# A graph attention and propagation kernel: a new order of the same instructions within a pipeline step

## The reference

```
h = x W_fc^T ;  f1 = h a1 ;  f2 = h a2
scores = leaky_relu(f1[:, None] + f2[None, :], 0.2), masked where adj == 0
attn = softmax(scores) ;  x = layernorm(x + elu(attn @ x))
xn = x / |x| ;  out = (xn xn^T) @ adj @ x ;  x = layernorm(x + out)
```

## Time and profile before

| what | value |
|---|---|
| median of three runs | 379.62 us |
| the profiled execution | 380.89 us, span 379.1 us |
| PE busy | 327.4 us (86%) |
| DVE busy | 330.5 us (87%) |
| ACT busy | 275.1 us (73%) |
| POOL busy | 194.7 us (51%) |
| moved by DMA | 42.41 MB, mean 112 GB/s |

### The profile page before, as it was taken

How to read it: one execution, slowest core, us unless ns; L and a number is a source line. 1 busy time by engine, 2 the same in 40 slices (tenths; PEclk the granted TensorE clock), 3 DMA queues, 4 the chain that set the end, 5 groups by cost and what they waited for, 6 DMA issues and landing times. The chain is left out here.

```text
span 379.1 us, 6926 instructions
## 1 busy us (share of the span) xinstructions
PE 327.4 (86%) x2244; PEld 302.6 (80%) x2244; DVE 330.5 (87%) x1012; ACT 275.1 (73%) x593; POOL 194.7 (51%) x167
## 2 busy tenths in 40 slices
PE   3095999899898989999898989989898989999790
PEld 1084999889797979889797979879797979998780
DVE  4589959999999999999999999999999999957412
ACT  0468696868878787868878787878878787884342
POOL 3405564654547375554548375554648475645401
PEclk9998799999999999999999999999999999999896
DMA  6861071534434544533443543633443541210102
GB/s 210 237 165 55 12 211 35 134 112 113 128 95 114 165 112 123 156 112 91 135 109 113 167 112 112 165 113 75 148 114 112 168 111 58 57 57 0 57 17 93
DMA packets 33971, 42.41 MB, mean 112 GB/s; under 512 B 1136, under 2 KB 25744, under 8 KB 33936
## 3 DMA queue, kind: packets, MB, share of 16 engines
q0 software_dynamic: 16896, 25.17, 24.6%
q1 hardware_dynamic: 17040, 16.81, 14.2%
HBM read 33.59 MB, written 8.39 MB: 111 GB/s over the span
## 5 line engine op out<-in xcount | busy, mean ns | idle before, releaser
L616 PE MATMUL ps_h<-x_hi,probT_hi 128*128 128x256 f32 x256 | 79.8, 312 | 0.4 <-issue 0.4
L617 PE MATMUL ps_h<-x_lo,probT_hi 128*128 128x256 f32 x256 | 72.8, 284 | 0.0
L618 PE MATMUL ps_h<-x_hi,probT_lo 128*128 128x256 f32 x256 | 72.6, 284 | 0.0
L600 PE MATMUL ps_probT<-ident,prob 128*128 128x128 f32 x256 | 41.6, 289 | 33.4 <-ACT prob L465 30.7
L646 PE MATMUL ps_l<-xn_hi,adj_sb 128*128 128x256 f32 x256 | 66.0, 297 | 2.1 <-POOL xn_lo L249 2.1
L600 PEld LDWEIGHTS ps_probT<-ident,prob 128*128 128x128 f32 x256 | 30.7, 148 | 43.8 <-ACT prob L465 35.2
L249 POOL TENSOR_TENSOR xn_lo<-xn,xn_hi 128x1024 fp32r<-128x1024 f32 x16 | 40.0, 2502 | 49.9 <-ACT xn_hi L499 49.9
L682 PE MATMUL ps_l<-w_sb,xnT 128*128 128x256 f32 x256 | 65.2, 380 | 0.3
L647 PE MATMUL ps_l<-xn_lo,adj_sb 128*128 128x256 f32 x256 | 63.3, 287 | 0.0
L669 PE MATMUL ps_l<-xn,z_sb 128*128 128x256 f32 x256 | 57.9, 379 | 0.0
L485 ACT ACTIVATE exp_h<-ps_h,rden 128x256 f32<-128x256 f32 x64 | 30.3, 474 | 36.9 <-PE ps_h L618 27.6
(11 more groups left out here) (52 smaller groups left out, 691.2 us busy)
## 6 DMA issues: line engine op xcount, KB each, us to landing
adj_sb<-adj POOLq DMA_DIRECT2D x16, 1024.0 KB, 5.9
x_sb<-x SPq DMA_DIRECT2D x16, 512.0 KB, 4.7
x_hi<-x POOLq DMA_DIRECT2D x16, 512.0 KB, 4.1
out<-o_sb SPq DMA_DIRECT2D x16, 512.0 KB, 3.1
attn_cols<-w_attn SPq DMA_DIRECT2D x2, 0.1 KB, 1.6
wfc<-w_fc SPq DMA_DIRECT2D x1, 32.0 KB, 1.7
```

Of the source, the lines that this page charges most:

```text
L600: last = nc.tensor.transpose(ps_probT[c % 2][:, k * P:(k + 1) * P], prob[:, c, k * P:(k + 1) * P], ident[:])
L616: nc.tensor.matmul(ps, probT_hi[:, c, blk], x_hi[n][:, k, :], start=(k == 0), stop=False)
L617: nc.tensor.matmul(ps, probT_hi[:, c, blk], x_lo[n][:, k, :], start=False, stop=False)
L618: last = nc.tensor.matmul(ps, probT_lo[:, c, blk], x_hi[n][:, k, :], start=False, stop=(k == NC - 1))
```

## The change

The four lists of calls are written in another order. Some calls change their index by one, as the loop's step boundary is at another place for that engine (on POOL `split_xn(i)` becomes `split_xn(i + 1)`, for example); each graph still gets each call once. `row_moments` and `row_moments2` are cut in two: the lines that add the epsilon are now functions of their own, `shifted_moments` and `shifted_moments2`, so that other calls can stand between. SP's list is as before. Waits, buffers, shapes and operations are the same.

```
 POOL
-                split_xn(i)
-                load_x_hi(i + 2)
-                norm(i)
                 load_adj(i + 3)
                 residual_sum(i + 1)
-                split_x(i + 2)
                 power2(i - 1)
+                load_x_hi(i + 3)
                 shift2(i - 1)
                 power(i + 1)
+                norm(i + 1)
+                split_xn(i + 1)
+                split_x(i + 3)

 DVE
                 last.then_inc(mv2_ok, 1)
+
+            def shifted_moments2(g):
+                if not graph(g):
+                    return
+                n = g % NBUF
                 dve.wait_ge(mv2_ok, g + 1)
...
-                residual2(i - 2, 1)
-                masked_f2(i + 1, 2)
-                negate_max(i + 1, 0)
+                masked_f2(i + 1, 3)
                 residual2(i - 2, 2)
                 residual2(i - 2, 3)
-                masked_f2(i + 1, 3)
-                node_scores(i + 2, 1)
+                negate_max(i + 1, 0)
+                negate_max(i + 1, 1)
+                node_scores(i + 2, 0)
                 residual(i)
-                negate_max(i + 1, 1)
                 row_moments2(i - 2)
                 probT_lo_part(i + 1, 0)
+                probT_lo_part(i + 1, 1)
+                shifted_moments2(i - 2)
                 row_moments(i)
-                node_scores(i + 2, 0)
-                probT_lo_part(i + 1, 1)
+                shifted_moments(i)
+                node_scores(i + 2, 1)
                 denominators(i + 1)
+                make_mask(i + 2)
                 normalise(i)
+                residual2(i - 1, 0)
                 probT_lo_part(i + 1, 2)
-                make_mask(i + 2)
+                masked_f2(i + 2, 0)
+                masked_f2(i + 2, 1)
                 probT_lo_part(i + 1, 3)
-                masked_f2(i + 2, 0)
-                residual2(i - 1, 0)
-                masked_f2(i + 2, 1)
+                masked_f2(i + 2, 2)
+                residual2(i - 1, 1)

 ACT (the new list; the old one is in the code above)
+                copy_xnT(i - 1, 0)
+                probT_hi_part(i + 1, 1)
+                lrelu(i + 1, 3)
+                copy_w(i - 1, 0)
+                copy_xnT(i - 1, 1)
+                softmax_exp(i + 1, 2)
+                softmax_exp(i + 1, 3)
+                copy_w(i - 1, 1)
+                normalise2(i - 2)
+                probT_hi_part(i + 1, 2)
+                elu_exp(i + 1, 0)
+                elu_relu(i + 1, 0)
+                elu_exp(i + 1, 1)
+                xn_hi_part(i)
+                probT_hi_part(i + 1, 3)
+                elu_relu(i + 1, 1)
+                lrelu(i + 2, 0)
+                elu_exp(i + 1, 2)
+                lrelu(i + 2, 1)
+                lrelu(i + 2, 2)
+                elu_relu(i + 1, 2)
+                elu_exp(i + 1, 3)
+                elu_relu(i + 1, 3)
+                scale_z(i, 0)
+                scale_z(i, 1)
+                softmax_exp(i + 2, 0)
+                softmax_exp(i + 2, 1)
+                scale_z(i, 2)
+                scale_z(i, 3)
+                probT_hi_part(i + 2, 0)

 PE (the new list)
+                bcast_f2(i + 1)
+                transpose_prob(i, 3)
                 attend(i, 2)
+                make_out(i - 2, 3)
                 attend(i, 3)
+                make_z(i - 1, 0)
+                make_z(i - 1, 1)
+                make_z(i - 1, 2)
+                make_z(i - 1, 3)
+                transpose_xn(i - 1, 0)
                 transpose_prob(i + 1, 0)
+                transpose_prob(i + 1, 1)
+                transpose_xn(i - 1, 1)
                 make_w(i - 1, 0)
                 make_w(i - 1, 1)
+                attend(i + 1, 0)
                 transpose_prob(i + 1, 2)
+                attend(i + 1, 1)
                 make_out(i - 1, 0)
                 make_out(i - 1, 1)
                 make_out(i - 1, 2)
```

More of the change, by code:

```diff
@@ L375, in row_moments, with shifted_moments @@
                 last.then_inc(mv_ok, 1)
+            def shifted_moments(g):
+                if not graph(g):
+                    return
+                n = g % NBUF
                 dve.wait_ge(mv_ok, g + 1)
@@ L539, in _ @@
             for i in STEPS:
[L540 to L556, removed]
                 copy_xnT(i - 1, 0)
-                softmax_exp(i + 1, 1)
+                probT_hi_part(i + 1, 1)
+                lrelu(i + 1, 3)
+                copy_w(i - 1, 0)
                 copy_xnT(i - 1, 1)
-                probT_hi_part(i + 1, 0)
-                copy_w(i - 1, 0)
                 softmax_exp(i + 1, 2)
-                lrelu(i + 1, 3)
+                softmax_exp(i + 1, 3)
                 copy_w(i - 1, 1)
-                probT_hi_part(i + 1, 1)
-                softmax_exp(i + 1, 3)
+                normalise2(i - 2)
                 probT_hi_part(i + 1, 2)
-                normalise2(i - 2)
                 elu_exp(i + 1, 0)
+                elu_relu(i + 1, 0)
[17 more added lines that the diff above has]
+                probT_hi_part(i + 2, 0)
         @block.tensor
@@ L686, in _ @@
             for i in STEPS:
+                bcast_f2(i + 1)
+                transpose_prob(i, 3)
                 attend(i, 2)
+                make_out(i - 2, 3)
                 attend(i, 3)
-                make_out(i - 2, 3)
-                for c in range(NC):
-                    make_z(i - 1, c)
+                make_z(i - 1, 0)
[3 more added lines that the diff above has]
+                transpose_xn(i - 1, 0)
                 transpose_prob(i + 1, 0)
-                for d in range(DC):
-                    transpose_xn(i - 1, d)
+                transpose_prob(i + 1, 1)
+                transpose_xn(i - 1, 1)
                 make_w(i - 1, 0)
                 make_w(i - 1, 1)
-                transpose_prob(i + 1, 1)
+                attend(i + 1, 0)
                 transpose_prob(i + 1, 2)
+                attend(i + 1, 1)
                 make_out(i - 1, 0)
-                attend(i + 1, 0)
                 make_out(i - 1, 1)
-                transpose_prob(i + 1, 3)
-                bcast_f2(i + 2)
-                attend(i + 1, 1)
                 make_out(i - 1, 2)
```

## The result

The changed kernel takes 357.01 us (median of 4 runs, 355.62 to 359.15) against 379.59: a ratio of 0.9415, 95% interval 0.9344 to 0.9486. In a second set it is 356.53 us, ratio 0.9425 (0.9387 to 0.9462). Forecast was 352 us in a range of 348 to 365.

What follows compares the result with a forecast made beforehand. DVE, held by POOL at L418, was taken to bound the kernel, with PE the bound afterwards. Twelve steps of 2.15 us, plus 2.6 at the end, minus 0.7 at the start, took 27.7 off 379.6: 352 us, range 348 to 365.

Steps and rivals of the forecast that it cites:

- The bound before was DVE, by a hold of L418: DVE is full in each 21.45 us step; its tiny epsilon addition takes 3.97 us, held while POOL works.
- PE becomes the bound, 19.3 us a step: With the new order PE never waits, so the step falls from 21.45 to 19.3 us.
- The floor: PE's own work per step: 21.45 less 2.16 us lost at two transposes of prob, 19.3 us.
- The hold at the new place: Moved shifted_moments2 on DVE meets POOL's residual sum: held 0 to 2.37 us, taken as 0.2.
- Early DVE part: Eight DVE operations reading PSUM run beside POOL's two splits; negate_max starts 4.8 to 5.4 us into the step.
- Late DVE part: DVE from node_scores to probT_lo 2, done at 19.2 us, needed by PE at 20.1; slack given as 0.7.
- The rule of the Trainium skill: Two-port or two-SBUF-input DVE instructions and SBUF-reading GpSimd ones block each other throughout; mask blocked until 15.8, sum unchanged.
- Start and end: Work before and after the twelve steps: start loses 0.7 us, allowing 4 either way; end gains 2.6.
- The sum: 12 x 2.15 + 2.6 - 0.7 = 27.7 us saved: span 351.4 us, median 352.
- adj lands late: Rival: adj, issued 6.8 us before its mask, arrives late; 380 to about 410 us; chance 0.03, plus 0.03 for no gain.
- Two holds for one: Rival: x_lo holds negate_max and residual sum holds L418; step 22.05 us, total 385; chance 0.05.
- DVE and POOL form the bound: Rival: an 18.2 us ring through DVE and POOL gains 1 to 3 us; total 354 to 372; chance 0.17.

Runs made afterwards that it cites:

- b_eps_late: Kernel before the change with only L418 and L419 moved behind row_moments(i) on DVE; 356.5 us, ratio 0.9404; timed again 355.4 us, ratio 0.936.
- v_o3_t2: Changed kernel with make_out(i - 2, 3) ahead of attend(i, 2) and transpose_prob(i + 1, 2) behind attend(i + 1, 1) on PE; 355.6 us, ratio 0.9413.
- a_eps_early: Changed kernel with L428 and L429 (L418 and L419 of before) put back directly behind row_moments2; 360.5 us, ratio 0.9509.
- b_xlo_late: Kernel before the change with POOL's x_lo split moved behind power2, shift2 and power; 444.4 us, ratio 1.1735.
- m_new_pe_act: Lists of before on DVE and POOL, new lists on PE and ACT; 426.2 us, ratio 1.1249 to the kernel before the change.

## Why the prediction was right, point by point

- **The bound before was DVE, by a hold of L418.** Right. b_eps_late moves L418 and L419 alone and gets everything; two ways of putting the hold back into the new order cost 3.5 and 17 us.
- **PE becomes the bound, 19.3 us a step.** Right; 19.42 measured, PE busy 100%. The 0.12 that is missing makes 1.4 us in twelve steps. It isn't the places where PE starts an attend from another kind of work (v_o3_t2 has two fewer). The floor was a difference, 21.45 less two lost times, and one of them was too large: T(3) was taken to be due 0.68 after the make_out at 186.01. That is what a make_out costs in front of an attend. In front of a transpose it is 0.86, as b_eps_late shows, where PE has the old list and waits for nothing:

```profile
212.89 1.03 PE L688 MATMUL ps_l<-w_sb,xnT 128*128 128x256 f32 x4
213.75 0.60 PE L606 MATMUL ps_probT<-ident,prob 128*128 128x128 f32 x4
```

  So 0.38 us was lost there and not 0.56. That would have put the floor at 19.47, 0.05 above the 19.42 measured and 0.07 above the 19.40 of b_eps_late.
- **The hold at the new place 0 to 2.37, taken as 0.2.** 0.4 us, and 0.7 at most.
- **Early DVE part under POOL's pair.** Right in order and nearly in time: negate_max 4.95 us after B's start (195.79 to 200.74), predicted 4.8 to 5.4, and the pair over by then. In the start it wasn't over twice, and one L334 lasted 2.4 us (at 44.1), another 0.85 (at 64.7).
- **Late DVE part.** probT_lo 2 was to end 0.7 us before A2 needs it; the times given for the two, 19.2 and 20.1, make 0.9. It ends at 195.6 and A2 starts at 196.6, 1.0 later, and the hold experiments put the slack at 1.0 too. DVE's wait before masked_f2 0 is 0.92 us (196.53 in the row above). Right in kind.
- **The rule of the Trainium skill** (SBUF — State Buffer, "Who interferes with whom"): the whole of the first operation, it says, and here the row before it showed two. The mask beside POOL's power is where it bears: power took 2.27 us instead of 1.74 and ended with the mask (191.96 + 1.20 = 193.16). So there is a hold where my row (node_scores beside power) had shown none, and in this the Trainium skill is right. But power started first (190.92, the mask at 191.96), so by the Trainium skill's rule the mask should have waited; it took 1.20 us, its normal time, and power was the one to end late. It cost nothing. In a_eps_early, where the mask comes 1.30 us after power, power takes 2.54 and again ends with it. Where the mask starts first, it is POOL that waits, as the rule has it. In b_eps_late xn_lo starts in the last 0.40 us of the mask and takes 2.67, in the earlier trace rows in the last 0.29 and takes 2.54; in the changed kernel no mask is beside it, and it takes 2.38:

```profile
216.21 1.22 DVE L307 TENSOR_SCALAR mask<-adj_sb 128x2048 bf16<-128x2048 f32 x1
```

```profile
217.03 2.67 POOL L249 TENSOR_TENSOR xn_lo<-xn,xn_hi 128x1024 fp32r<-128x1024 f32 x1 [2.75 <-ACT xn_hi L505]
```

- **Start and end.** B(3) at 59.5 (said 59.7), end 60.9 us after B(15) (said 60.1). That the start is hit so closely is partly luck: in the second profile of the same kernel B(3) is at 62.0. At the end the last xn_lo was to start 34.4 us after B(15) and starts 35.2 after it. Most of this is a wait that the layout left out: normalise is done at 326.4, but ACT is in normalise2 and starts xn_hi at 327.0.
- **The sum.** Span: 1.8 for the twelve steps (233.4 us between B(3) and B(15), said 231.6), 0.8 at the end, -0.2 at the start: 353.8 instead of 351.4. Of the 1.8, 0.4 lie in the first of the twelve, which takes 19.81. The other part of the 5 us in the median comes from executions that differ. I took the median to stand to the profiled execution as before (1.3 under it); it stands 1.4 over it. The two profiled executions have spans of 353.8 and 356.5, and the masks waited for adj twice in each, for graph 0 (3.0 and 3.3 us) and for graph 3, 1.4 us in the one and 3.1 in the other. In total, times and longest:

```profile
DVE mask L307 <- DMA adj_sb<-adj: 4.4, 2, 3.0
```

```profile
DVE mask L307 <- DMA adj_sb<-adj: 6.4, 2, 3.3
```

  The second has B(3) 2.5 us later, a first step of 21.55, and so B(15) 4.2 us later (297.1); its end is 1.5 shorter (59.4), with a granted clock of 1.00 instead of 0.95 in the second 20 us behind B(15). So the rival "adj lands late" came in a place where I hadn't put it, the start, once. It explains part of the difference between the executions; the rest is open. The median of 357.0 lies at the edge of what was given for a kernel bound by PE (348 to 357), though the steady step is PE-bound throughout.
- **Rivals.** "Two holds for one" didn't happen in the steady part of the changed kernel; a_eps_early has it, with holds of 0.83 and 1.62. "DVE and POOL form the bound" didn't, but a_eps_early, at 19.67 with a hold of 1.6, shows how near it was.
- **What the prediction gave too much weight:** it laid out all four lists and took the whole new order for the cause. It didn't ask which part of it was enough. The rest of the new order is worth nothing that these runs can show.

## What to carry to other kernels

Look for an instruction that lasts far longer than its kind, with no semaphore to blame, and put the other engine's timeline beside it: the end of the neighbour's operation says who holds it. Then try to move the held instruction alone, behind work that isn't held, before touching the rest; a producer that is moved instead takes its readers with it, and in b_xlo_late a late input, with what followed from it, cost more than the hold had. When lists of several engines have been written to suit one another, a new list for one of them can be slower than either whole set.

## What the runs showed of the hardware that I had not expected

- A DVE instruction on four numbers, caught in the first of two POOL operations in a row, a sum and a subtraction, waited for both (3.97 us; 4.4 in m_new_pe_act), whether its form was tensor_scalar or scalar_tensor_tensor. Where no second one followed (b_xlo_late) it waited for one, 1.66.
- The hold works the other way too: POOL's power on eight numbers grew from 1.74 to 2.27 us (2.54 in a_eps_early) and ended with the DVE mask beside it, and xn_lo grew from 2.38 to 2.67 when it started in the last 0.40 us of a mask.
- bn_stats (1.39 us for four), masked_f2 with one operand in PSUM (0.68), and probT_lo (0.69) ran at their own speed beside the same POOL subtractions.
- PE, kept waiting 3.9 us in a step of b_xlo_late, had a granted clock of 0.898 over the profiled execution, against 0.969 to 0.989 in those of all the others.
